# A small fp32 product on TensorE becomes one transpose, with the sums taken by VectorE

## The chip, the cores and the metric

One core of a Trainium2 chip. The metric is the time of one execution on the device in microseconds (us), median of several runs. "The loop" below is the edge loop of the graph attention, which runs once in each of two layers.

## What is computed

`x` has 1250 nodes of 768 features. The reference adds to it a two-layer graph attention over 41250 directed edges and a linear attention, and then a feed-forward block. The change is in the graph attention, whose core is this:

```python
hs_e = hs[src]
e = jax.nn.leaky_relu(hs_e + hd[dst], SLOPE)
logits = jnp.einsum('ehd,hd->eh', e, attn)       # 8 heads of 96
m = jax.ops.segment_max(logits, dst, num_segments=N)
ex = jnp.exp(logits - m[dst])
s = jax.ops.segment_sum(ex, dst, num_segments=N)
out = jax.ops.segment_sum((ex / s[dst])[..., None] * hs_e, dst, num_segments=N)
```

## The kernel before

Edges are sorted by destination and cut into tiles of 128; four tiles make a **macro**, and there are 91 macros in a layer. For every macro the kernel gathers four tiles of source rows by indirect DMA, turns them (six chunks of 128 features, four tiles each) and adds the destinations' rows on TensorE in PSUM (`turn_chunk`), takes the relu on ScalarE (`bend`, one 128x512 activation per chunk), joins three pairs of chunks on VectorE (`join`), sums over the features of each head on TensorE (`sum_heads`), and scans over the edges on VectorE (`scan_left`, `scan_right`, `shift`) to subtract a running maximum. The shifted logits are turned back (`turn_back`), ScalarE takes their exponential (`weights`), VectorE spreads them into a masked matrix (`spread_out`), and TensorE multiplies that with the gathered rows (`messages`). VectorE adds the result to the running sums of the destination blocks (`add_total`, two instructions for each of the four tiles).

A running maximum may rise between macros. By how much is the column `rise` of 128 partitions: a partition is tile j times 32 plus a head's place, h // 4 times 4 plus h % 4. ScalarE makes `drop` from it (`drops`), TensorE sums and places it for the partitions that `sums` has (`sum_drops`), and ScalarE takes the exponentials of it (`factors`, four activations of 128x2), by which `add_total` scales what was summed so far. `quarter_mask` is a 128x8 mask of zeros and ones, `head_rows` a 128x128 one.

The loop is pipelined by hand into slots: in a slot, TensorE does the messages of macro i, `sum_heads` and what follows for macro i + 1 (`head`), and turns the chunks of macro i + 2 (`turn`). In each layer 88 of the slots run as 22 rounds of a loop of four, the rest is written out. TensorE's order in a slot is fixed: messages, heads (products of chunk 3, of chunk 5, of chunk 4), chunks 0, 1, 2, `turn_back`, chunks 3, 4, `sum_drops`, `turn_linear`, chunk 5. ScalarE's is: relu 0, linear, relu 1, `weights`, `drops`, relu 2, 3, 4, `factors`, relu 5. VectorE's is: three joins, one tile's additions, the scans and the shift, three tiles' additions, `spread_out`. Engines meet through semaphores that count; among these, `sum_heads` waits before its second product, that of chunk 5, for relu 5.

Of the kernel before, what the change touches and what calls it, by code (L numbers as in the profile page):

```python
# [15 lines left out]
P = 128  # L16
# [13 lines left out]
HM = 4  # L30
HH = H // HM
# [327 lines left out]
JOINED = ((0, 1), (2, 3), (1, 4))  # L359
JOINED_HEADS, ALONE, LEAST = (3, 4), 5, 3  # L360
LOOPS = (NM - TAIL) // UNROLL
assert LOOPS * UNROLL + TAIL == NM
# [14 lines left out]
def macro(i, k):  # L377
# [5 lines left out]
              "turned_back", "weights_ready", "spread_ready", "totalled", "added", "firsts", "merge_ready", "merged",  # L383
              "merge_seen", "joined", "linear_ready")
AT_LISTS = ("local_loaded", "flags_loaded", "lines_loaded", "gathered")
# [20 lines left out]
def attend(layer, ahead, sums, table, places, lines, run_flags, src_index, first_dst, still_first, block_of, sum_of,  # L406
           ident, head_rows, quarter_mask, dst_rows, sems, nc, **_):

    with ExitStack() as ctx:
# [3 lines left out]
        def psum(name):  # L413
# [8 lines left out]
        right, shifted = sb("at_right", [P, P]), sb("at_shifted", [P, P])  # L422
        drop = sb("at_drop", [P, G * HH])
        weight = sb("at_weight", [P, G * H])
# [15 lines left out]
        (cleared, index_ready, index_seen, turned_done, bent, heads_done, scanned, raised, dropped, turned_back, weights_ready,  # L440
         spread_ready, totalled, added, firsts, merge_ready, merged, merge_seen, joined, linear_ready) = sems[0:len(AT_SIGNALS)]
        local_loaded, flags_loaded, lines_loaded, gathered = (
# [11 lines left out]
        with nc.Block() as block:  # L454
# [71 lines left out]
            def _(act):  # L526
# [6 lines left out]
                def drops(m, b):  # L533
                    act.wait_ge(scanned, m * SCANS + (SCANS + 2))
                    act.activation(rise[:], left[(b + 1) % 2][:, P - 1:P], ACT.Identity, bias=right[:, 0:1], scale=-1.0)
                    act.activation(first_maxima[:, bass.ds(m, 1)], right[:, 0:1], ACT.Copy).then_inc(raised, 1)
                    act.wait_ge(raised, m + 2)
                    act.activation(drop[:], quarter_mask[:, 0], ACT.Relu, scale=rise[:]).then_inc(dropped, 1)

# [5 lines left out]
                def factors(m, b):  # L545
                    act.wait_ge(turned_back, 2 * m + 2)
                    for j in range(G):
                        act.activation(factor[b % 2][:, j, :], back[:, P + j * HH:P + (j + 1) * HH], ACT.Exp,  # L548
                                       scale=first_dst[:, bass.ds(m * G + j, 1)]).then_inc(weights_ready, 1)
# [37 lines left out]
            def _(pe):  # L587
# [46 lines left out]

                def sum_drops(m):
                    weights_there, drop_there = count(m * EXPS + (EXPS + 1)), count(m + 1)
                    pe.wait_ge(weights_ready, weights_there)
                    pe.wait_ge(dropped, drop_there)
                    pe.matmul(back[:, P:P + G * HH], head_rows[:], drop[:], start=True, stop=True).then_inc(turned_back, 1)  # L639

# [21 lines left out]
                def slot(turn, head, message, at, coming=None):  # L662
                    if message:
                        for pair in range(2):
                            messages(message[0], message[1], pair)
                    if head:
                        sum_heads(head[0], head[1])
                    if turn:
                        turn_chunk(*turn, at, 0)
                        turn_chunk(*turn, at, 1)  # L670
                        turn_chunk(*turn, at, 2)
                    if head:
                        turn_back(head[0])
                    following = None
                    if turn:
                        turn_chunk(*turn, at, 3)
                        if coming:
                            following = coming(turn[0] + 1)
                        turn_chunk(*turn, at, 4)
                    if head:  # L680
                        sum_drops(head[0])
                    if turn:
                        turn_linear(turn[0])
                        turn_chunk(*turn, at, 5)
                    return following
# [19 lines left out]
            def _(dve):  # L705
# [22 lines left out]
                def spread_out(m, b, round):  # L728
# [3 lines left out]
                                      weight[:].rearrange("p (j h) -> p j h", j=G).unsqueeze(3).broadcast_to([P, G, H, S]), ALU.mult).then_inc(spread_ready, 1)  # L732

                def add_total(m, b, j, at):
                    dve.wait_ge(totalled, m * 2 + (j // 2 + 1))
# [8 lines left out]
                def slot(head, message):  # L744
                    if message:
                        at = places_of(nc, mybir.EngineType.DVE, sum_of, message[0], 1, NS + G - 1)
                    if head:
                        for k in range(len(JOINED)):
                            join(head[0], k)
                    if message:  # L750
                        for j in range(1):
                            add_total(message[0], message[1], j, at)
# [4 lines left out]
                    if message:  # L757
                        for j in range(1, G):
                            add_total(message[0], message[1], j, at)
# [1633 lines left out]
```

## Time and profile before

| | |
|---|---|
| time, median of 3 runs | 2142.82 us (2141.51 to 2144.17) |
| profiled execution, its own time | 2140.68 us |
| its span, first to last instruction | 2138.9 us |
| TensorE matmul busy | 2052.9 us, 96% |
| VectorE busy | 1641.7 us, 77% |
| ScalarE busy | 1160.9 us, 54% |
| GpSimd busy | 975.4 us, 46% |
| mean granted TensorE clock | 0.986 |

The span lies within the execution's own time; the 1.8 us between are before the first and after the last instruction. PE is TensorE's matmul, PEld its weight load, DVE is VectorE, ACT ScalarE, POOL GpSimd. A busy share is a mean over all stages: how long a slot of the loop takes is read from the start of an instruction in one slot to the start of the same one in the next.

### The profile page before, as it was taken

The page shows a single profiled execution, that of the slowest core. Times are in us where ns is not written, and L with a number is a line of the kernel's source. Part 1 is how long each engine was busy: PE and PEld are TensorE (multiplying, and loading weights), DVE is VectorE, ACT ScalarE, POOL GpSimd, SP SyncE. Part 2 cuts the span into 40 slices and gives each one's busy share as a digit, 9 for nine tenths or more (in the row PEclk, how much of TensorE's full clock was granted, in tenths as well). Part 3 has the DMA queues.
Part 4 walks back from the last instruction along what each step waited for, and adds up shares of the span by engine and source line. Part 5 has one row for each costly group of instructions (what it writes and reads, how often), then busy time and mean ns, then how long its engine had stood idle before and what let it go on. Part 6 is the DMA issues. An engine that isn't in the chain of part 4 may idle for free. (4 is left out here: it accounts for less than half of the span.)

```text
span 2138.9 us, 85423 instructions
## 1 busy us (share of the span) xinstructions
PE 2052.9 (96%) x29551; PEld 1665.6 (78%) x29552; DVE 1641.7 (77%) x3719; ACT 1160.9 (54%) x3113; POOL 975.4 (46%) x1023
## 2 busy tenths in 40 slices
PE   7999999998999999999998899899999999999798
PEld 4665555555899999999997555599999999999676
DVE  5545883554799999999998764499999999999883
ACT  2101210014677777777775413477777777777583
POOL 0000010110677777777772311277777777777020
PEclk9999999999999999999999999999999999999899
DMA  6000233683888888888884224488888888888511
GB/s 202 1 0 16 74 105 121 185 208 78 248 270 269 274 270 270 271 268 272 270 273 136 87 91 128 131 264 272 269 270 272 271 263 275 271 266 275 185 49 51
DMA packets 184668, 415.48 MB, mean 194 GB/s; under 512 B 59967, under 2 KB 122693, under 8 KB 184557
## 3 DMA queue, kind: packets, MB, share of 16 engines
q0 software_dynamic: 59584, 298.64, 45.0%
q1 hardware_dynamic: 105899, 98.97, 14.9%
q10 hardware_dynamic: 19104, 16.79, 2.8%
q8 instruction: 50, 0.82, 0.2%
q14 instruction: 31, 0.25, 0.0%
HBM read 379.72 MB, written 23.13 MB: 188 GB/s over the span
## 5 line engine op out<-in xcount | busy, mean ns | idle before, releaser
L531 ACT ACTIVATE at_relu<-at_turned,ah_attn_size 128x512 f32<-128x512 f32 x1092 | 713.9, 688 | 306.4 <-PE at_turned L605 286.6
L507 POOL DMA_INDIRECT at_rows<-table,ah_index x360 | 425.2, 1181 | 175.9 <-POOL ah_index L495 71.7
L507 POOL DMA_INDIRECT ah_room<-table,ah_index x352 | 422.8, 1201 | 164.7 <-POOL ah_index L495 65.7
L711 DVE SCALAR_TENSOR_TENSOR at_relu<-at_relu,ah_pair_sign 128x512 f32<-128x512 f32 x546 | 376.8, 744 | 8.2 <-ACT at_relu L531 8.2
L741 DVE SCALAR_TENSOR_TENSOR sums<-sums,at_factor,at_total 128x97 f32 x1456 | 358.8, 308 | 5.4 <-PE at_total L647 2.2
L601 PE MATMUL at_turned<-ident,ah_room 128*128 128x128 f32 x2208 | 341.1, 277 | 19.3 <-PEq L1702 19.0
L601 PE MATMUL at_turned<-ident,at_rows 128*128 128x128 f32 x2160 | 331.0, 276 | 0.1
L601 PEld LDWEIGHTS at_turned<-ident,ah_room 128*128 128x128 f32 x2208 | 243.3, 142 | 40.5 <-issue 40.3
L601 PEld LDWEIGHTS at_turned<-ident,at_rows 128*128 128x128 f32 x2160 | 236.3, 141 | 19.9 <-issue 19.9
L731 DVE TENSOR_TENSOR at_spread<-at_lined,at_weight 128x1024 f32<-128x1024 bf16 x182 | 221.5, 1217 | 2.8 <-ACT at_weight L542 2.8
L605 PE MATMUL at_turned<-ah_place,dst_rows 96*128 96x128 bf16 x2208 | 215.7, 219 | 0.0
L605 PE MATMUL at_turned<-at_place,dst_rows 96*128 96x128 bf16 x2160 | 209.9, 219 | 0.1
L605 PEld LDWEIGHTS at_turned<-ah_place,dst_rows 96*128 x2208 | 171.8, 98 | 6.6
L605 PEld LDWEIGHTS at_turned<-at_place,dst_rows 96*128 x2160 | 167.0, 97 | 6.5 <-issue 0.4
L717 DVE TENSOR_TENSOR_SCAN at_left<-at_flags,at_left,at_heads 128x128 f32<-128x128 bf16 x182 | 87.2, 479 | 98.4 <-PE at_heads L617 96.9
L617 PE MATMUL at_heads<-at_relu,ah_sign_mask 128*8 128x128 f32 x4368 | 153.6, 273 | 1.2 <-ACT at_relu L531 0.5
L647 PE MATMUL at_total<-ah_room,at_spread 128*32 128x100 f32 x5888 | 145.4, 250 | 0.9 <-issue 0.2
L647 PE MATMUL at_total<-at_rows,at_spread 128*32 128x100 f32 x5760 | 143.6, 252 | 1.4 <-DVE at_spread L731 1.4
L647 PEld LDWEIGHTS at_total<-ah_room,at_spread 128*32 128x32 f32 x5888 | 125.3, 110 | 13.0 <-issue 7.4
L548 ACT ACTIVATE at_factor<-at_back,first_dst 128x2 f32<-128x2 f32 x728 | 132.4, 281 | 1.3 <-PE at_back L639 1.3
L647 PEld LDWEIGHTS at_total<-at_rows,at_spread 128*32 128x32 f32 x5760 | 123.5, 110 | 10.8 <-DVE at_spread L731 1.6
L617 PEld LDWEIGHTS at_heads<-at_relu,ah_sign_mask 128*8 128x8 f32 x4368 | 107.8, 89 | 9.7 <-ACT at_relu L531 1.1
(315 smaller groups left out, 2884.7 us busy)
## 6 DMA issues: line engine op xcount, KB each, us to landing
at_flags<-run_flags SPq DMA_DIRECT2D x182, 64.0 KB
dst_rows<-pr_parts SPq DMA_DIRECT2D x76, 144.0 KB, 2.7
ah_place<-places SPq DMA_DIRECT2D x92, 96.0 KB
at_place<-places SPq DMA_DIRECT2D x90, 96.0 KB
table<-ah_room SPq DMA_DIRECT2D x20, 400.0 KB, 3.2
ah_room<-table,ah_index POOLq DMA_INDIRECT x368
at_lined<-lines SPq DMA_DIRECT2D x182, 32.0 KB
at_rows<-table,ah_index POOLq DMA_INDIRECT x360
```

The source lines that it names most:

```text
L507: pool.indirect_dma_start(rows[b][:, j, :], None, table, bass.IndirectOffsetOnAxis(index[b][:, j:j + 1], 0)).then_inc(gathered[b], 16)
L531: act.activation(relu[c][:], turned[chunk(b, c)][:], ACT.Relu, scale=attn_size[:, c:c + 1]).then_inc(bent, 1)
L548: act.activation(factor[b % 2][:, j, :], back[:, P + j * HH:P + (j + 1) * HH], ACT.Exp, scale=first_dst[:, bass.ds(m * G + j, 1)]).then_in ...
L601: pe.matmul(into[j], rows[b][:, j, c * P:(c + 1) * P], ident[:], is_transpose=True, start=j == 0, stop=False)
L605: last = pe.matmul(into[j], dst_rows[0:SP_ROWS, bass.ds(at[j], 1), c * P:(c + 1) * P].rearrange("p o d -> p (o d)"), place[b][:, j * P:(j ...
L617: last = pe.matmul(head_row(j), sign_mask[:, c - LEAST, :], relu[c][:, j * P:(j + 1) * P], start=False, stop=final)
L647: last = pe.matmul(part(j)[h % HM * S:(h % HM + 1) * S, h // HM, :], spread[:, j, h, :], rows[b][:, j, :].rearrange("p (g h r) -> p h g r" ...
L711: dve.scalar_tensor_tensor(relu[c][:], relu[from_][:], pair_sign[:, c:c + 1], relu[c][:], ALU.mult, ALU.add).then_inc(joined, 1)
L717: dve.tensor_tensor_scan(left[b % 2][:], flags[b][:, 0, :], heads[:, 0:P], left[(b + 1) % 2][:, P - 1:P], ALU.add, ALU.max).then_inc(scann ...
L731: dve.tensor_tensor(spread[:], lined[b % 2][:].unsqueeze(2).broadcast_to([P, G, H, S]), weight[:].rearrange("p (j h) -> p j h", j=G).unsqu ...
L741: dve.scalar_tensor_tensor(into[:, k], into[:, k], factor[b % 2][:, j, k:k + 1], part(j)[:, k, 0:HW], ALU.mult, ALU.add).then_inc(added, 1)
```

## The change

`drop` grows from 128x8 to 128x128 (it now lies in `iota_row`, a 128x128 tile of fp32 that is there already), `sum_drops` becomes `turn_drops`, a transpose of it, and a new VectorE instruction, `fold_drops`, adds groups of four columns of the transposed tile in PSUM and writes 128x8 numbers, `fold`, to SBUF. `factors` now waits for that (`folded`) and reads `fold` in SBUF, where it read `back` in PSUM. In VectorE's slot the new instruction stands between the first and the second join, and the second tile's additions move ahead of the scans.

```diff
+AHEAD_OF_SCANS = 2
...
-        drop = sb("at_drop", [P, G * HH])
+        drop, fold = iota_row, sb("at_fold", [P, G, HH])
...
-                    act.activation(drop[:], quarter_mask[:, 0], ACT.Relu, scale=rise[:]).then_inc(dropped, 1)
+                    act.activation(drop[:], head_rows[:], ACT.Relu, scale=rise[:]).then_inc(dropped, 1)
...
                 def factors(m, b):
-                    act.wait_ge(turned_back, 2 * m + 2)
+                    act.wait_ge(folded, m + 1)
                     for j in range(G):
-                        act.activation(factor[b % 2][:, j, :], back[:, P + j * HH:P + (j + 1) * HH], ACT.Exp,
+                        act.activation(factor[b % 2][:, j, :], fold[:, j, :], ACT.Exp,
                                        scale=first_dst[:, bass.ds(m * G + j, 1)]).then_inc(weights_ready, 1)
...
-                def sum_drops(m):
+                def turn_drops(m):
                     weights_there, drop_there = count(m * EXPS + (EXPS + 1)), count(m + 1)
                     pe.wait_ge(weights_ready, weights_there)
                     pe.wait_ge(dropped, drop_there)
-                    pe.matmul(back[:, P:P + G * HH], head_rows[:], drop[:], start=True, stop=True).then_inc(turned_back, 1)
+                    pe.transpose(back[:, P:2 * P], drop[:], ident[:]).then_inc(turned_back, 1)
...
+                def fold_drops(m):
+                    dve.wait_ge(turned_back, 2 * m + 2)
+                    dve.tensor_reduce(fold[:], back[:, P:2 * P].rearrange("p (j k g) -> p j k g", j=G, g=HM)[:, :, 0:HH, :], AX.X, ALU.add).then_inc(folded, 1)
...
                     if head:
-                        for k in range(len(JOINED)):
-                            join(head[0], k)
+                        join(head[0], 0)
                     if message:
-                        for j in range(1):
+                        fold_drops(message[0])
+                    if head:
+                        join(head[0], 1)
+                        join(head[0], 2)
+                    if message:
+                        for j in range(AHEAD_OF_SCANS):
                             add_total(message[0], message[1], j, at)
                     if head:
                         scan_left(*head)
                         scan_right(head[0], head[1])
                         shift(head[0])
                     if message:
-                        for j in range(1, G):
+                        for j in range(AHEAD_OF_SCANS, G):
                             add_total(message[0], message[1], j, at)
```

TensorE, in one of the loop's slots, between chunks 4 and 5: the product with `at_drop` as its moving side (fp32, two passes in the trace), before,

```order
L605 MATMUL at_turned_0<-at_place_0,dst_rows 128x128
L637 ISA
L639 MATMUL at_back<-at_drop,head_rows 128x8 [waits at_dropped,at_weights_ready]
L612 MATMUL at_heads<-ident,at_linear 128x128 [waits at_linear_ready]
L599 REGISTER_ALU
```

and now, with the same waits:

```order
L606 MATMUL at_turned_0<-at_place_0,dst_rows 128x128
L638 ISA
L640 MATMUL at_back<-ident,iota_row 128x128 [waits at_dropped,at_weights_ready]
L613 MATMUL at_heads<-ident,at_linear 128x128 [waits at_linear_ready]
L600 REGISTER_ALU
```

One instruction stands in the place of one; nothing else moves on TensorE.

VectorE, in one of the loop's slots, from the first join to the first scan (`at_relu_0` are the relu tiles, `sums` the running sums), before,

```order
L711 SCALAR_TENSOR_TENSOR at_relu_0<-at_relu_0,ah_pair_sign 128x512 [waits at_bent]
L708 REGISTER_ALU
L711 SCALAR_TENSOR_TENSOR at_relu_0<-at_relu_0,ah_pair_sign 128x512 [waits at_bent]
...
L711 SCALAR_TENSOR_TENSOR at_relu_0<-at_relu_0,ah_pair_sign 128x512 [waits at_joined]
...
L741 SCALAR_TENSOR_TENSOR sums<-sums,at_factor_0,at_total_0 128x97
L741 ISA
L741 SCALAR_TENSOR_TENSOR sums<-sums,at_factor_0,at_total_0 128x97
L714 REGISTER_ALU
L717 SCALAR_TENSOR_TENSOR at_left_0<-at_flags_0,at_left_0,at_heads 128x128 [waits at_flags_loaded3,at_raised,at_heads_done]
```

and now:

```order
L712 SCALAR_TENSOR_TENSOR at_relu_0<-at_relu_0,ah_pair_sign 128x512 [waits at_bent]
L736 ISA
L737 TENSOR_REDUCE at_fold<-at_back 128x8 [waits at_turned_back]
L709 REGISTER_ALU
L712 SCALAR_TENSOR_TENSOR at_relu_0<-at_relu_0,ah_pair_sign 128x512 [waits at_bent]
...
L746 SCALAR_TENSOR_TENSOR sums<-sums,at_factor_0,at_total_0 128x97
L746 ISA
L746 SCALAR_TENSOR_TENSOR sums<-sums,at_factor_0,at_total_0 128x97
L746 ISA [waits at_totalled]
L746 SCALAR_TENSOR_TENSOR sums<-sums,at_factor_0,at_total_0 128x97
L746 ISA
```

The reduction stands behind the first join, and four additions instead of two stand ahead of the scan; behind the shift there are four instead of six.

## Rows read from the trace of the kernel before

**Rows 1.** Page: busy time by engine; the costliest groups of lines.

```profile
PE 2052.9 (96%) x29551; PEld 1665.6 (78%) x29552; DVE 1641.7 (77%) x3719; ACT 1160.9 (54%) x3113; POOL 975.4 (46%) x1023
...
L617 PE MATMUL at_heads<-at_relu,ah_sign_mask 128*8 128x128 f32 x4368 | 153.6, 273 | 1.2 <-ACT at_relu L531 0.5
```

**Rows 2.** Timeline of TensorE, one slot: start us, length us, instructions.

```profile
705.33 0.28 PE L633 MATMUL at_back<-ident,at_shifted 128*128 128x128 f32 x1
705.45 0.60 PE L601 MATMUL at_turned<-ident,ah_room 128*128 128x128 f32 x4
...
706.78 0.34 PE L639 MATMUL at_back<-at_drop,head_rows 128*128 128x8 f32 x2
706.97 0.31 PE L612 MATMUL at_heads<-ident,at_linear 128*128 128x128 f32 x1
707.12 0.27 PE L601 MATMUL at_turned<-ident,ah_room 128*128 128x128 f32 x1
...
709.27 0.49 PE L617 MATMUL at_heads<-at_relu,ah_sign_mask 128*8 128x128 f32 x9
...
709.27 0.84 PE L617 MATMUL at_heads<-at_relu,ah_sign_mask 128*8 128x128 f32 x24
```

**Rows 3.** Timeline of ScalarE, the same slot.

```profile
704.78 0.25 ACT L554 ACTIVATE at_linear<-ah_room 128x32 f32<-128x32 f32 x1
704.94 0.67 ACT L531 ACTIVATE at_relu<-at_turned,ah_attn_size 128x512 f32<-128x512 f32 x1
705.65 0.20 ACT L542 ACTIVATE at_weight<-at_back 128x32 f32<-128x32 f32 x1
705.74 0.29 ACT L535 ACTIVATE at_columns<-at_left,at_right 128x1 f32<-128x1 f32 x1
705.94 0.19 ACT L536 ACTIVATE at_first_maxima<-at_right 128x1 f32 x1
706.16 0.30 ACT L538 ACTIVATE at_drop<-quarter_mask,at_columns 128x8 f32<-128x8 f32 x1
706.36 1.83 ACT L531 ACTIVATE at_relu<-at_turned,ah_attn_size 128x512 f32<-128x512 f32 x3
708.07 0.73 ACT L548 ACTIVATE at_factor<-at_back,first_dst 128x2 f32<-128x2 f32 x4
708.65 0.73 ACT L531 ACTIVATE at_relu<-at_turned,ah_attn_size 128x512 f32<-128x512 f32 x1
```

**Rows 4.** Timeline of the loop's first slot, where TensorE waits for relu 5.

```profile
544.47 0.41 PE L617 MATMUL at_heads<-at_relu,ah_sign_mask 128*8 128x128 f32 x8
545.12 0.28 PE L617 MATMUL at_heads<-at_relu,ah_sign_mask 128*8 128x128 f32 x1 [0.25 <-ACT at_relu L531]
...
543.61 1.47 ACT L531 ACTIVATE at_relu<-at_turned,ah_attn_size 128x512 f32<-128x512 f32 x2
```

**Rows 5.** Timeline, next slot, around the loop's branch: TensorE, ScalarE, VectorE.

```profile
712.09 0.28 PE L633 MATMUL at_back<-ident,at_shifted 128*128 128x128 f32 x1
...
716.09 0.41 PE L617 MATMUL at_heads<-at_relu,ah_sign_mask 128*8 128x128 f32 x8
...
715.41 0.73 ACT L531 ACTIVATE at_relu<-at_turned,ah_attn_size 128x512 f32<-128x512 f32 x1
...
712.81 1.22 DVE L731 TENSOR_TENSOR at_spread<-at_lined,at_weight 128x1024 f32<-128x1024 bf16 x1
```

**Rows 6.** Timeline of ScalarE behind the loop, and in the last stage (out of PSUM).

```profile
1159.84 0.28 ACT L535 ACTIVATE at_columns<-at_left,at_right 128x1 f32<-128x1 f32 x1
1160.03 0.19 ACT L536 ACTIVATE at_first_maxima<-at_right 128x1 f32<-128x1 f32 x1
...
2050.95 0.86 ACT L2145 ACTIVATE fi_hidden<-fi_hidden_ps,fi_bias 128x128 f32<-128x128 f32 x3
...
L2145 ACT ACTIVATE fi_hidden<-fi_hidden_ps,fi_bias 128x128 f32<-128x128 f32 x30 | 8.8, 362 | 7.3 <-PE fi_hidden_ps L2204 7.2
```

**Rows 7.** Timeline of VectorE, the slot of rows 2; then the groups by shape.

```profile
705.94 1.22 DVE L731 TENSOR_TENSOR at_spread<-at_lined,at_weight 128x1024 f32<-128x1024 bf16 x1
707.08 2.07 DVE L711 SCALAR_TENSOR_TENSOR at_relu<-at_relu,ah_pair_sign 128x512 f32<-128x512 f32 x3
709.13 0.54 DVE L741 SCALAR_TENSOR_TENSOR sums<-sums,at_factor,at_total 128x97 f32 x2
710.28 0.48 DVE L717 TENSOR_TENSOR_SCAN at_left<-at_flags,at_left,at_heads 128x128 f32<-128x128 bf16 x1 [0.61 <-PE at_heads L617]
...
L711 DVE SCALAR_TENSOR_TENSOR at_relu<-at_relu,ah_pair_sign 128x512 f32<-128x512 f32 x546 | 376.8, 744 | 8.2 <-ACT at_relu L531 8.2
L741 DVE SCALAR_TENSOR_TENSOR sums<-sums,at_factor,at_total 128x97 f32 x1456 | 358.8, 308 | 5.4 <-PE at_total L647 2.2 <-DVE at_relu L794 0.7 <-issue 0.2
...
L1076 DVE TENSOR_REDUCE quarter_mask<-ident 128x8 f32<-128x32 f32 x1 | 0.2, 176 | 0.0
```

More of the change, by code:

```diff
@@ L383 @@
               "turned_back", "weights_ready", "spread_ready", "totalled", "added", "firsts", "merge_ready", "merged",
-              "merge_seen", "joined", "linear_ready")
+              "merge_seen", "joined", "linear_ready", "folded")
 AT_LISTS = ("local_loaded", "flags_loaded", "lines_loaded", "gathered")
@@ L406, in attend @@
 def attend(layer, ahead, sums, table, places, lines, run_flags, src_index, first_dst, still_first, block_of, sum_of,
-           ident, head_rows, quarter_mask, dst_rows, sems, nc, **_):
+           iota_row, ident, head_rows, quarter_mask, dst_rows, sems, nc, **_):
     with ExitStack() as ctx:
@@ L440, in attend @@
         (cleared, index_ready, index_seen, turned_done, bent, heads_done, scanned, raised, dropped, turned_back, weights_ready,
-         spread_ready, totalled, added, firsts, merge_ready, merged, merge_seen, joined, linear_ready) = sems[0:len(AT_SIGNALS)]
+         spread_ready, totalled, added, firsts, merge_ready, merged, merge_seen, joined, linear_ready, folded) = sems[0:len(AT_SIGNALS)]
         local_loaded, flags_loaded, lines_loaded, gathered = (
@@ L680, in slot @@
                     if head:
-                        sum_drops(head[0])
+                        turn_drops(head[0])
                     if turn:
```

## The prediction

> **What bounds the kernel now.** The page of the profile comes first: TensorE's matmuls are busy for 96% of the span, VectorE for 77%, ScalarE for 54% [rows 1]. So a cut on TensorE looks like the only cut that pays. But a busy share doesn't say how close the others follow behind it, so I read one slot of the loop in the timeline, TensorE's and ScalarE's rows side by side. Reader: look for the place at which TensorE needs something from ScalarE, and how long before that it was there.
>
> From one `turn_back` (705.33 us) to the next (712.09) a slot takes 6.76 us [rows 2, 5], with hardly a gap on TensorE. ScalarE's work in a slot starts from that `turn_back`: its exponential stands at 705.65, directly behind the product's end at 705.33 + 0.28 = 705.61 [rows 2, 3]. From there `weights`, `rise`, the copy of the maxima, `drop`, relu 2, 3 and 4, four factors and relu 5 follow each other without a pause, and relu 5 ends at 708.65 + 0.73 = 709.38 [rows 3]. TensorE needs it at the ninth matmul of `sum_heads`. Nine of these matmuls end 0.49 after 709.27, and one lasts 0.27, so the ninth starts at 709.49 [rows 2]. Relu 5 is there 0.10 us (0.103 by the records' own times) before its use. How much of that is free? In the loop's first slot TensorE does wait for it: relu 5 ends at 543.61 + 1.47 = 545.08 and the matmul starts at 545.12 (0.05 apart, unrounded 0.053) [rows 4]. So **the slack is 0.05 us per slot**: over the whole trace TensorE waits 0.5 us in these groups for ScalarE [rows 1], yet ScalarE is almost a second critical path, from `turn_back` to the ninth matmul of `sum_heads`. The removed product lies on TensorE inside that same stretch.
>
> **The change, part by part.**
>
> TensorE. The product of two passes takes from 706.78 to 706.97, and the linear transpose behind it until 707.12: 0.34 together. A single fp32 transpose, `turn_back`, takes 705.33 to 705.45, 0.12 [rows 2]; two such in a row make 0.24. Saving: 0.10 us per slot (bounds: 0.07 if only the product's own 0.19 shrinks to 0.12, and 0.10), or 18 us over 182 slots if nothing else ended later.
>
> ScalarE, `drop`. It has 128 columns instead of 8. The price of a column: relus of 512 columns start (708.07 - 706.36) / 3 = 0.570 apart, factors of 2 columns (708.65 - 708.07) / 4 = 0.145 apart [rows 3], so 0.425 / 510 = 0.83 ns. The 128-column activations of the last stage confirm it: three take 0.86, one 0.36 in the mean, so they start 0.25 apart [rows 6], and 0.145 + 126 x 0.83 ns = 0.25. So 120 columns more are **+0.10 us**. The 0.20 between `drop` and relu 2 could hide part of it, if register work and not the activation set it: then 0.04 is the low bound. I take 0.10, since the last row of this kind without such work fits as well: `rise` (1 column, SBUF, a per-partition operand) is followed after 0.19 by the copy behind the loop, 0.20 within it [rows 3, 6], the same as behind `drop`.
>
> ScalarE, `factors`. They are as many and as wide as before, but read SBUF instead of PSUM, with a per-partition scale from SBUF. The rows divide by this: `rise`, out of SBUF and with such an operand, keeps the engine 0.185 to 0.20 us for one column [rows 3, 6]; a factor, out of PSUM and with such an operand, 0.145; `weights`, out of PSUM and without one, 0.09 for 32 columns, and the linear copy, out of SBUF and without one, 0.16 for 32 [rows 3]. So SBUF as the source costs some 0.04 to 0.055 more per activation, four times: **+0.16 to +0.22**, low bound 0 (if `rise` owes its spacing to something else). I take 0.18. Against it stands that relu 5 lasts 0.73 behind the factors and 0.67 where nothing is queued closely ahead of it [rows 3]: its start is recorded early while results pile up, and with wider spacing it won't be; -0.04.
>
> The Trainium skill (ScalarE: Activation LUTs, "What ACT_TABLE_LOAD costs") gives 186 ns plus 0.833 ns per column, 93 more for each per-partition operand, and an overlap of 93 between neighbours. By that a factor takes 0.19 wherever it reads. The `rise` row agrees; the factors' own 0.145 doesn't, and the row decides. Taken as it stands the rule would leave the factors' price unchanged, and this is the first rival.
>
> The wait for `folded`. VectorE's first join starts at 707.08, three joins of 0.74 end after 2.07, so they start 0.66 apart: the reduction can start at 707.74. The same shape was reduced once from SBUF in 0.18 [rows 7]; it ends at 707.92. From one engine's end to another's start with register work between I take 0.17 (the heads' products end at 709.27 + 0.84 = 710.11 [rows 2], the scan starts at 710.28 [rows 7]): 708.09. ScalarE reaches the factors at 708.07 + 0.10 for the wider `drop` = 708.17. So the wait is covered by `drop`'s own growth, by 0.08. In the slot after, `spread_out` starts 0.72 behind `turn_back` instead of 0.61 [rows 2, 5, 7], which would use the cover up; but there VectorE was late with its additions, and with four of them behind the shift instead of six (0.23 each: two end after 0.54, one lasts 0.31) it will wait for `weights` alone. Price 0, bounds 0 and 0.1.
>
> VectorE itself. The reduction pushes the next joins by under 0.2, and two additions more stand ahead of the scan. It idles 0.61 there now [rows 7], and the two additions are 0.46. The factors come 0.1 + 0.14 later, so the additions start at about 709.37 instead of 709.13 and leave the engine free at 710.29; but `sum_heads` ends later too, by what TensorE waits. The scan starts where it did, behind `sum_heads`. The joins have 0.3 us and more left before their products. Price 0.
>
> **The sum.** Relu 5 comes 0.10 + 0.18 - 0.04 = 0.24 us later, measured from `turn_back`. An ordinary slot has 0.05 of slack, so it grows by 0.19: TensorE waits 0.29 at the ninth matmul and had saved 0.10. One slot in four, at the loop's branch, has more: relu 5 ends at 716.14, the ninth matmul starts at 716.09 + 0.22 = 716.31, 0.17 apart, 0.12 of it free [rows 5]; it grows by 0.12. A round: 3 x 0.19 + 0.12 = 0.69. 44 rounds: 30 us; the six slots outside add 1, and the few rounds in which TensorE was late in this stretch for other reasons take off 2. **+29 us.** Against the profiled execution's own 2140.7 that is 2169.7. That execution lies 2.1 below the median of the runs shown, 2142.8; against the median I forecast 2172.
>
> **Rivals.**
> First, the factors cost no more out of SBUF than out of PSUM. Relu 5 is late by 0.10 alone; an ordinary slot grows by 0.05, one at the branch shrinks by 0.02: 44 x 0.13 = 6 us, 2148. For it: nothing but `rise` and `drop` price SBUF with an operand at few columns. Against: both rows say the same, with and without register work.
>
> Second, **faster**: ScalarE's growth doesn't reach relu 5 because `drop`'s is hidden in register work and the factors' spacing stays. It is the place of the sum with the hardest cap: TensorE can gain only the slack of 0.05 in an ordinary slot and the full 0.10 at a branch, 44 x 0.25 = 11 us, 2132. It decides when relu 5 is late by under 0.05 in place of 0.24. Against: the slope of 0.83 ns is in three kinds of rows.
>
> Third, the fold is late. If VectorE's reduction of PSUM or its place behind the join costs 0.2 more than I take, all factors start 0.1 later and every slot with them: 18 us more, 2190.
>
> **How the numbers follow.** The forecast (both ScalarE terms, late by 0.16 to 0.32; 2157 to 2186) has 0.65; the first rival 0.15, of which a third lies within 0.2%; the second 0.08, a little of it within 0.2%; the third 0.12. A change of under 0.2% is about what a measurement of this kernel can't tell from none. Faster 0.07, same 0.07, slower 0.86. The range leaves out the second rival and the upper part of the third: 2147 to 2187.
>
> **What would show it.** In the profile after: `drop` at 0.40 us instead of 0.30; factors' starts 0.185 to 0.20 apart, the four taking some 0.85 from first to last end; a wait of TensorE in `sum_heads` on the relu, 0.2 to 0.3 us per slot, 45 us or so in all, where there are 0.5 now; the transpose 0.12 before the linear one; slots of 6.95 instead of 6.76; VectorE no longer late for `spread_out`. Wrong would be: factors 0.145 apart (then the first rival), no wait in `sum_heads` (the second), ScalarE idle ahead of the factors waiting for `fold` (the third), or a scan that starts behind the additions and not behind `sum_heads`.

## The result, and the profile after

| | before | after |
|---|---|---|
| time, median | 2142.2 us (2141.5 to 2144.2, 4 runs) | 2169.6 us (2167.1 to 2169.7, 4 runs) |
| profiled execution, own time / span | 2140.7 / 2138.9 us | 2169.5 / 2167.8 us |
| TensorE / VectorE / ScalarE busy | 96 / 77 / 54% | 95 / 78 / 55% |

The ratio is 1.0123 (95% interval 1.0112 to 1.0135): the changed kernel is 1.2% slower. 2172 was forecast, 29 us up; it is 27. One run of experiment 1 fell into a slow state (2347 us, at a lower granted clock, 0.864); its ratio leaves that run out.

The page after, the busy times and the groups that answer to [rows 1], with the two groups of the changed instructions on ScalarE and the new one on VectorE:

```profile
PE 2068.6 (95%) x29369; PEld 1643.4 (76%) x29370; DVE 1681.7 (78%) x3901; ACT 1201.2 (55%) x3113; POOL 1009.2 (47%) x1023
...
L618 PEld LDWEIGHTS at_heads<-at_relu,ah_sign_mask 128*8 128x8 f32 x4368 | 102.0, 89 | 55.0 <-ACT at_relu L532 46.4
...
L539 ACT ACTIVATE iota_row<-head_rows,at_columns 128x128 f32<-128x128 f32 x182 | 73.2, 402 | 5.9
...
L549 ACT ACTIVATE at_factor<-at_fold,first_dst 128x2 f32<-128x2 f32 x728 | 154.5, 294 | 8.1 <-DVE at_fold L737 8.1
...
L737 DVE TENSOR_REDUCE at_fold<-at_back 128x8 f32<-128x32 f32 x182 | 33.5, 184 | 1.0 <-DVE at_relu L803 1.0
```

The line to look at is the weight load of `sum_heads` (L618): TensorE now waits 46.4 us there for the relu. The same row of the kernel before, and the row of the group's matmuls after, which [rows 1] has for before:

```profile
L617 PEld LDWEIGHTS at_heads<-at_relu,ah_sign_mask 128*8 128x8 f32 x4368 | 107.8, 89 | 9.7 <-ACT at_relu L531 1.1
...
L618 PE MATMUL at_heads<-at_relu,ah_sign_mask 128*8 128x128 f32 x4368 | 186.1, 273 | 9.5 <-ACT at_relu L532 0.5
```

Like is compared with like in the weight loads: 1.1 us before, 46.4 after. The 0.5 that the prediction read stands in the matmuls' row, and it is 0.5 after as well, so that row could not have shown the wait. TensorE's busy time went up in the page though a pass was taken from it. These matmuls are recorded as 273 ns long, before and after, but in an undisturbed group they start closely behind each other and their records overlap. When the ninth comes 0.25 us later, the record of the eighth covers most of the gap, and the group counts as 186.1 us busy instead of 153.6. Busy time alone tells the wrong story.

One ordinary slot, TensorE, from the timeline (answers to [rows 2]):

```profile
709.18 0.28 PE L634 MATMUL at_back<-ident,at_shifted 128*128 128x128 f32 x1
709.30 0.60 PE L602 MATMUL at_turned<-ident,ah_room 128*128 128x128 f32 x4
...
710.63 0.28 PE L640 MATMUL at_back<-ident,iota_row 128*128 128x128 f32 x1
710.74 0.27 PE L613 MATMUL at_heads<-ident,at_linear 128*128 128x128 f32 x1
710.85 0.60 PE L602 MATMUL at_turned<-ident,ah_room 128*128 128x128 f32 x4
...
713.00 0.78 PE L618 MATMUL at_heads<-at_relu,ah_sign_mask 128*8 128x128 f32 x9
...
716.11 0.28 PE L634 MATMUL at_back<-ident,at_shifted 128*128 128x128 f32 x1
```

ScalarE in the same slot (answers to [rows 3]):

```profile
709.50 0.20 ACT L543 ACTIVATE at_weight<-at_back 128x32 f32<-128x32 f32 x1
...
710.01 0.40 ACT L539 ACTIVATE iota_row<-head_rows,at_columns 128x128 f32<-128x128 f32 x1
710.32 1.82 ACT L532 ACTIVATE at_relu<-at_turned,ah_attn_size 128x512 f32<-128x512 f32 x3
712.03 0.84 ACT L549 ACTIVATE at_factor<-at_fold,first_dst 128x2 f32<-128x2 f32 x4
712.77 0.68 ACT L532 ACTIVATE at_relu<-at_turned,ah_attn_size 128x512 f32<-128x512 f32 x1
```

VectorE in the same slot (answers to [rows 7]):

```profile
709.73 1.23 DVE L732 TENSOR_TENSOR at_spread<-at_lined,at_weight 128x1024 f32<-128x1024 bf16 x1 [0.30 <-ACT at_weight L543]
710.87 0.74 DVE L712 SCALAR_TENSOR_TENSOR at_relu<-at_relu,ah_pair_sign 128x512 f32<-128x512 f32 x1
711.53 0.18 DVE L737 TENSOR_REDUCE at_fold<-at_back 128x8 f32<-128x32 f32 x1
711.63 1.41 DVE L712 SCALAR_TENSOR_TENSOR at_relu<-at_relu,ah_pair_sign 128x512 f32<-128x512 f32 x2
713.12 0.99 DVE L746 SCALAR_TENSOR_TENSOR sums<-sums,at_factor,at_total 128x97 f32 x4
714.30 0.48 DVE L718 TENSOR_TENSOR_SCAN at_left<-at_flags,at_left,at_heads 128x128 f32<-128x128 bf16 x1 [0.19 <-PE at_heads L618]
```

Read in this order: from `turn_back` to `turn_back` 709.18 to 716.11, 6.93 us instead of 6.76. The drops' transpose and the linear one take 0.22 (710.63 to 710.85) instead of 0.34, so TensorE did save 0.12. ScalarE reaches relu 2 0.31 behind the start of `drop` instead of 0.21 (0.207 unrounded), and its factors start 0.185 apart ((712.77 - 712.03) / 4) instead of 0.145. Relu 5 ends at 713.45, 4.27 behind `turn_back` instead of 4.05. The ninth matmul of `sum_heads` starts at 713.00 + 0.78 - 0.27 = 713.51, 0.06 (0.053 unrounded) behind relu 5: exactly the distance that [rows 4] showed for the slot in which TensorE waited. The fold ends at 711.71, 0.3 ahead of the factors.

### The profile page after: what moved, and what is told of

Read it like the earlier page. It is cut to its first block and busy times, and to the rows that moved or that the text cites. A ratio compares the mean times of both kernels' runs of the same rounds, so it can differ in the third digit from the quotient of the medians.

```text
span 2167.8 us, 85066 instructions
## 1 busy us (share of the span) xinstructions
PE 2068.6 (95%) x29369; PEld 1643.4 (76%) x29370; DVE 1681.7 (78%) x3901; ACT 1201.2 (55%) x3113; POOL 1009.2 (47%) x1023
## 5 line engine op out<-in xcount | busy, mean ns | idle before, releaser
L532 ACT ACTIVATE at_relu<-at_turned,ah_attn_size 128x512 f32<-128x512 f32 x1092 | 705.2, 680 | 291.9 <-PE at_turned L606 284.2
L508 POOL DMA_INDIRECT at_rows<-table,ah_index x360 | 444.8, 1236 | 172.1 <-issue 82.1
L508 POOL DMA_INDIRECT ah_room<-table,ah_index x352 | 435.4, 1237 | 162.3 <-issue 68.6
L712 DVE SCALAR_TENSOR_TENSOR at_relu<-at_relu,ah_pair_sign 128x512 f32<-128x512 f32 x546 | 391.7, 745 | 9.1 <-ACT at_relu L532 9.1
L618 PE MATMUL at_heads<-at_relu,ah_sign_mask 128*8 128x128 f32 x4368 | 186.1, 273 | 9.5 <-ACT at_relu L532 0.5
L549 ACT ACTIVATE at_factor<-at_fold,first_dst 128x2 f32<-128x2 f32 x728 | 154.5, 294 | 8.1 <-DVE at_fold L737 8.1
L618 PEld LDWEIGHTS at_heads<-at_relu,ah_sign_mask 128*8 128x8 f32 x4368 | 102.0, 89 | 55.0 <-ACT at_relu L532 46.4
```

What stands on the lines that cost most here:

```text
L508: pool.indirect_dma_start(rows[b][:, j, :], None, table, bass.IndirectOffsetOnAxis(index[b][:, j:j + 1], 0)).then_inc(gathered[b], 16)
L532: act.activation(relu[c][:], turned[chunk(b, c)][:], ACT.Relu, scale=attn_size[:, c:c + 1]).then_inc(bent, 1)
L549: act.activation(factor[b % 2][:, j, :], fold[:, j, :], ACT.Exp, scale=first_dst[:, bass.ds(m * G + j, 1)]).then_inc(weights_ready, 1)
L618: last = pe.matmul(head_row(j), sign_mask[:, c - LEAST, :], relu[c][:, j * P:(j + 1) * P], start=False, stop=final)
L712: dve.scalar_tensor_tensor(relu[c][:], relu[from_][:], pair_sign[:, c:c + 1], relu[c][:], ALU.mult, ALU.add).then_inc(joined, 1)
```

## The experiments

All times are medians; ratios are against the kernel before, run beside each. Unless said otherwise a kernel starts from the changed one.

**1. The wide drop alone.** On the kernel before; `drop` is a view of the same 128x128 tile.

```diff
-                    act.activation(drop[:], quarter_mask[:, 0], ACT.Relu, scale=rise[:])
+                    act.activation(drop, over(quarter_mask[:, 0], P // (G * HH)), ACT.Relu, scale=rise[:])
...
-                    pe.matmul(back[:, P:P + G * HH], head_rows[:], drop[:], start=True, stop=True)
+                    pe.matmul(back[:, P:P + G * HH], head_rows[:], drop[:, 0], start=True, stop=True)
```

> The kernel before, with one edit: ScalarE writes drop as 128x128 (the 128x8 mask repeated 16 times), of which TensorE's product reads the first 8 columns. Nothing else changes. My theory (the path turn_back, ScalarE, relu 5, sum_heads bounds the slot, with 0.05 us of slack): drop lasts 0.40, relu 2 starts 0.31 behind it instead of 0.21, relu 5 comes 0.10 later, an ordinary slot grows by 0.05 and one at the loop's branch not at all: about +7 us, 2149 against 2142. Rival (register work hides the wider drop): +0 to 1 us. Rival (only the wait for the fold or VectorE's order costs): no change.

Measured: 2150.0 against 2143.1, ratio 1.0031 (1.0019 to 1.0043). ScalarE's rows:

```profile
706.40 0.40 ACT L538 ACTIVATE iota_row<-quarter_mask,at_columns 128x128 f32<-128x128 f32 x1
706.71 1.82 ACT L531 ACTIVATE at_relu<-at_turned,ah_attn_size 128x512 f32<-128x512 f32 x3
708.42 0.72 ACT L548 ACTIVATE at_factor<-at_back,first_dst 128x2 f32<-128x2 f32 x4
708.99 0.73 ACT L531 ACTIVATE at_relu<-at_turned,ah_attn_size 128x512 f32<-128x512 f32 x1
```

Relu 2 starts 0.31 behind `drop`: the columns' full 0.10 is paid, no register work hides it. The +7 us are those of my theory.

**2. The factors from SBUF alone.** `drop` is 128x8 again and the product stands as before; VectorE copies its 128x8 result. Of the edit, the lines of TensorE and VectorE:

```diff
-                    pe.transpose(back[:, P:2 * P], drop[:], ident[:])
+                    pe.matmul(back[:, P:P + G * HH], head_rows[:], drop[:], start=True, stop=True)
...
-                    dve.tensor_reduce(fold[:], back[:, P:2 * P].rearrange("p (j k g) -> p j k g", j=G, g=HM)[:, :, 0:HH, :], AX.X, ALU.add)
+                    dve.tensor_copy(fold[:], back[:, P:P + G * HH].rearrange("p (j k) -> p j k", j=G))
```

> The changed kernel with the drops as before (128x8, product on TensorE); VectorE copies the product's 128x8 from PSUM to SBUF where the changed kernel adds, and the factors read the copy in SBUF. VectorE's order is the changed one. My theory: factors start 0.185 apart instead of 0.145 (4 x 0.04 = 0.16), relu 5 lasts 0.68 instead of 0.73, so relu 5 comes 0.11 later, an ordinary slot grows by 0.06 and one at the branch hardly: about +8 us, 2150; up to +6 more if the factors now wait for the copy, which has lost the cover of the wider drop. Rival (the source of the factors costs nothing): +0 us but for such a wait.

Measured: 2153.5 against 2143.1, ratio 1.0050 (1.0036 to 1.0064).

```profile
706.00 1.83 ACT L532 ACTIVATE at_relu<-at_turned,ah_attn_size 128x512 f32<-128x512 f32 x3
707.71 0.85 ACT L549 ACTIVATE at_factor<-at_fold,first_dst 128x2 f32<-128x2 f32 x4
708.45 0.68 ACT L532 ACTIVATE at_relu<-at_turned,ah_attn_size 128x512 f32<-128x512 f32 x1
```

The factors follow relu 4 as closely as before (1.71 behind the start of relu 2, as in [rows 3]), so no wait for the copy stands in; they start 0.185 apart. In the loop's slots the source alone costs this: from the first to the last `turn_back` the two layers take 9.3 us more. Some 1.4 us more lie at the ends of the layers (see the wait for the fold below).

**3. The fold in PSUM.** VectorE writes the fold into another part of `back`'s bank.

```diff
-        drop, fold = iota_row, sb("at_fold", [P, G, HH])
+        drop = iota_row
...
+        fold = back[:, 2 * P:2 * P + G * HH].rearrange("p (j k) -> p j k", j=G)
```

> The changed kernel, but VectorE writes the fold to PSUM (another part of the same bank), and the factors read it there. My theory: factors 0.145 apart again, relu 5 0.11 earlier than in the changed kernel; TensorE's saving of 0.12 stays; slots of 6.82: about 2150, 20 us faster than the changed kernel and 7 slower than the kernel before. Rival (the cost is the wait for the fold, or its place in VectorE's queue): no faster than the changed kernel, 2169.

Measured: 2151.0 against 2143.1, ratio 1.0032 (1.0021 to 1.0043); 8 us over the kernel before, where the changed kernel is 27 over it.

```profile
709.36 1.82 ACT L533 ACTIVATE at_relu<-at_turned,ah_attn_size 128x512 f32<-128x512 f32 x3
711.07 0.73 ACT L550 ACTIVATE at_factor<-at_back,first_dst 128x2 f32<-128x2 f32 x4
711.65 0.73 ACT L533 ACTIVATE at_relu<-at_turned,ah_attn_size 128x512 f32<-128x512 f32 x1
```

Same instructions, same waits, same order; only the memory in which the fold's 128x8 numbers lie differs, and it decides: 0.145 apart again, and relu 5 lasts 0.73 again. The rival (a wait for the fold, its place in VectorE's queue) falls as the cause of the 19 us between these two kernels.

**4. TensorE's part alone.** On the kernel before; the rises are left out of the sums.

```diff
-                    pe.matmul(back[:, P:P + G * HH], head_rows[:], drop[:], start=True, stop=True)
+                    pe.transpose(back[:, P:2 * P], head_rows[:], ident[:])
```

> TensorE's part alone: the kernel before, in which TensorE transposes the 128x128 mask in place of the product with drop; ScalarE and VectorE are as before, and the factors read the first columns of that transpose. The rises of the maxima are left out of the sums, so the output isn't the reference's. My theory (TensorE can gain no more than the slack of 0.05 in an ordinary slot, 0.12 at the branch): 12 us faster, 2130. Rival (TensorE alone bounds the slot, 0.12 in each): 21 us faster, 2121.

Measured: 2136.4 against 2143.1, ratio 0.9969 (0.9958 to 0.9980), 7 us faster where 12 were expected and 21 by the rival. The waits of the whole trace:

```profile
PEld at_heads L617 <- ACT at_relu L531: 15.7, 91, 0.5
```

This view counts 91 waits of TensorE for relu 5, where the kernel before had two (1.1 us): the slack of 0.05 is used up, as expected, and an ordinary slot takes 6.71. What I had wrong is the slot at the loop's branch: it stays at about 6.85, and doesn't gain the 0.12 that was expected. Experiments 6 to 12 come back to this.

**5. VectorE's order.** One tile's additions ahead of the scans again.

```diff
-AHEAD_OF_SCANS = 2
+AHEAD_OF_SCANS = 1
```

> The changed kernel with one tile's additions ahead of the scans, as before, instead of two. My theory (VectorE's order isn't on the path that sets the end): no change against the changed kernel, 2169, within 2. Rival (the second tile's additions ahead of the scan delay what follows): faster by up to their 0.46 us per slot.

Measured: 2172.2 against 2142.6, ratio 1.0139 (1.0124 to 1.0155); the changed kernel's own ratio was 1.0123 (1.0112 to 1.0135). The intervals overlap. The order isn't a cause of the loss, and two ahead gain nothing that these runs can tell.

**6. Relu 5 first.** ScalarE takes relu 5 ahead of the factors; one tile's additions ahead of the scans.

```diff
+                        bend(turn[0], turn[1], 5, first)
                     if head:
                         factors(head[0], head[1])
-                    if turn:
-                        bend(turn[0], turn[1], 5, first)
...
-AHEAD_OF_SCANS = 2
+AHEAD_OF_SCANS = 1
```

> The changed kernel with relu 5 ahead of the four factors on ScalarE, and one tile's additions ahead of the scans. My theory: relu 5 ends some 0.75 earlier, far ahead of its use, so TensorE bounds the slot and its 0.12 comes through wherever the loop's branch doesn't take it: 16 us faster than the kernel before, 2127. The factors end 0.7 later, which delays the first additions to 0.3 behind the end of sum_heads; the scan's 0.55 of slack before turn_back covers that. Rival (VectorE is then the bound): slots of 6.8 and more, 2143 or slower.

Measured: 2140.1 against 2142.6, ratio 0.9989 (0.9980 to 0.9998). This is 29 us less than the changed kernel, and the only kernel with the whole computation that is also under the kernel before, by 2.5 us (the interval ends just below 1). Since the order of the additions makes no difference (5), relu 5's lateness was the whole loss. But of the 16 us expected below the kernel before, 2.5 came. `turn_back` of five consecutive slots, and the wait of the whole trace that shows where time is lost:

```profile
706.40 0.28 PE L633 MATMUL at_back<-ident,at_shifted 128*128 128x128 f32 x1
...
713.05 0.28 PE L633 MATMUL at_back<-ident,at_shifted 128*128 128x128 f32 x1
...
720.00 0.28 PE L633 MATMUL at_back<-ident,at_shifted 128*128 128x128 f32 x1
...
726.65 0.28 PE L633 MATMUL at_back<-ident,at_shifted 128*128 128x128 f32 x1
...
733.41 0.28 PE L633 MATMUL at_back<-ident,at_shifted 128*128 128x128 f32 x1
...
PEld at_total L647 <- issue: 13.7, 42, 0.5
```

6.65, 6.95, 6.65, 6.76: two slots in four have the full gain of 0.11, the one at the branch takes 6.95 instead of 6.83, and the fourth 6.76. The 42 waits "for issue" (the profile shows nothing that TensorE waited for) all lie in the slots at the branch, ahead of the messages. A round of four takes 27.0 (medians of the positions: 6.96 + 6.65 + 6.75 + 6.65), against 27.1 before (6.83 + 3 x 6.76). Number 4 comes to the same 27.0 with other slots (6.85 + 3 x 6.71). What is gained in some slots is lost in the others.

**7. One factor activation.** VectorE multiplies by `first_dst`, ScalarE takes one exponential of 128x8.

```diff
-                    for j in range(G):
-                        act.activation(factor[b % 2][:, j, :], fold[:, j, :], ACT.Exp,
-                                       scale=first_dst[:, bass.ds(m * G + j, 1)]).then_inc(weights_ready, 1)
+                    act.activation(factor[b % 2][:], fold[:], ACT.Exp).then_inc(weights_ready, 1)
...
-                    dve.tensor_reduce(fold[:], back[:, P:2 * P]... AX.X, ALU.add).then_inc(folded, 1)
+                    dve.tensor_reduce(fold[:], back[:, P:2 * P]... AX.X, ALU.add).then_inc(summed, 1)
+                    dve.wait_ge(summed, m + 1)
+                    dve.tensor_tensor(fold[:], fold[:], first_dst[:, bass.ds(m * G, G)].unsqueeze(2).broadcast_to([P, G, HH]), ALU.mult).then_inc(folded, 1)
```

> The changed kernel, in which VectorE multiplies the fold by first_dst as well (one 128x8 instruction more, behind the reduction), so that one activation of 128x8 replaces the four factors. My theory: ScalarE's path is shorter by some 0.6, relu 5 ends about 3.65 behind turn_back, TensorE doesn't wait for it: 2127. Rival (the fold's wait costs what the factors give back): 2140 and over.

Measured: 2142.8 against 2142.6, ratio 1.0003 (0.9994 to 1.0012). Relu 5 ends 3.65 behind `turn_back`, as expected, and TensorE doesn't wait for it; but 2127 was expected, and the time is that of before all the same, with the same pattern of slots as in 6 (a round of 27.1). The rival here, a wait for the fold, isn't the reason: relu 5 comes as early as expected.

**8. Both of these.** One tile's additions ahead of the scans.

> Both of these edits together, with one tile's additions ahead of the scans. My theory: TensorE is the bound in each of them already, so the two together give no more than the faster of them, within 3 us. Rival (some of the path is still ScalarE's or VectorE's): faster than both by over 3 us.

Measured: 2145.0 against 2142.6, ratio 1.0010 (1.0001 to 1.0019). That is no better than 6 or 7, and 5 us slower than 6, where at most 3 us apart were expected. One row of its waits:

```profile
PEld at_heads L615 <- DVE at_relu L709: 19.4, 95, 0.3
```

TensorE now waits for VectorE's joins, 19.4 us in 95 slots, where the kernels of 6 and 7 have 0.6 and 0.7 us; its best slots take 6.70 instead of 6.65. So ScalarE's path doesn't hold the rest, but this run can't acquit VectorE. The traces of 6 and 7 can: TensorE waits there neither for the relu nor for the joins in more than a few slots, and a round takes 27.0 and 27.1.

**9 to 11. A longer loop for TensorE.** Eight slots per round, TensorE alone: on 6, on the kernel before, and on the changed one.

```diff
-                with pe.Fori(0, LOOPS) as i:
+                with pe.Fori(0, LOOPS // 2) as i:
                     at = carried_blocks()
-                    for k in range(UNROLL):
-                        at = slot(macro(i, k + 2), macro(i, k + 1), macro(i, k), at, blocks if k < UNROLL - 1 else carry_blocks)
+                    for n in range(2 * UNROLL):
+                        two = [(i * (2 * UNROLL) + k, k % UNROLL, i * 2 + k // UNROLL) for k in (n + 2, n + 1, n)]
+                        at = slot(*two, at, blocks if n < 2 * UNROLL - 1 else carry_blocks)
```

> Of the kernel with relu 5 ahead of the factors, TensorE's loop alone has eight slots per round instead of four, so half the branches; the instructions are the same. In that kernel the slots away from the branch are at 6.65, those at the branch at 6.96 (0.20 of it ahead of the messages), and a round of four takes 27.0 as before the change. Theory A (a branch costs TensorE a fixed time, which now shows): 22 branches fewer per layer, 0.2 to 0.35 each: 9 to 15 us faster than with four, 2125 to 2131. Theory B (TensorE can't start instructions faster than this in the mean, wherever the branch is): no change, 2140.

> The kernel before, with TensorE's loop of eight slots per round. Slots at the branch take 0.07 more than the others there: theory A gives 2 to 3 us faster, 2140; theory B no change.

> The changed kernel, with TensorE's loop of eight slots per round. All its slots take 6.93, the ones at the branch too, since ScalarE's path from turn_back to relu 5 sets them: no change, 2170, under both theories of the branch. If the branch did set the slots there: 2 us faster and more.

Measured: 2309.1, 2306.0 and 2327.7 against 2143.0; ratios 1.0789 (1.0769 to 1.0808), 1.0783 (1.0762 to 1.0803), 1.0865 (1.0849 to 1.0881). All three expectations were wrong by 158 us and more, in the same way, so these runs don't answer what they were made for. From number 10: the queue that carries instructions (packets, MB, share); the messages behind one long wait and, a slot later, without one; the window right behind that wait, whose last three numbers are the mean granted clock, DMA share and GB/s; and all such waits:

```profile
q8 instruction: 293, 4.80, 0.9%
...
801.12 2.90 PE L647 MATMUL at_total<-ah_room,at_spread 128*32 128x100 f32 x64 [5.61 <-issue]
...
809.60 1.58 PE L647 MATMUL at_total<-ah_room,at_spread 128*32 128x100 f32 x64
...
801.10:805.00 3.90, 3.88 (x89) 3.51 (x90) 0.54 (x2) 0.00 (x0) 0.09 (x1) 0.59 0.04 14
...
PEld at_total L647 <- issue: 99.2, 23, 5.9
```

The queue has 293 packets instead of 50, 4.80 MB instead of 0.82. The 243 more are 11 for each of the 22 rounds (11 in each layer), and the kernel has 23 waits of 99 us in all ahead of the messages' weight loads in which nothing of the profile holds TensorE. A second loss follows: after the 5.6 us of idleness TensorE's granted clock is 0.59 of full speed in the mean of the next 3.9 us, and the 64 matmuls of the messages last 2.90 us instead of 1.58. It is so behind 19 of the 20 waits of over 1 us, some 25 us in all for the messages alone. The Trainium skill (Runtime: NRT & Kernel Launch, "Instruction fetch mechanics") says that TensorE's instruction memory holds 128 KiB and is filled in blocks of 16 KiB, and that a taken branch whose target isn't in the current window must fetch it first. The traces agree with the blocks and the fetch: the packets are 16 KB each (3.98 MB / 243), and a loop twice as long costs them in each round. A run with six slots, which would find the limit, wasn't made.

**12. Without TensorE's address registers.** On 6: destination blocks 0 to 3 for every macro, so the register work ahead of each of 24 matmuls per slot and the loads of the numbers are left out of TensorE's program. The destinations' rows are then the wrong ones, so the output isn't the reference's; the matmuls are the same. Of the edit, the main line:

```diff
-                        last = pe.matmul(into[j], dst_rows[0:SP_ROWS, bass.ds(at[j], 1), c * P:(c + 1) * P]...
+                        last = pe.matmul(into[j], dst_rows[0:SP_ROWS, j:j + 1, c * P:(c + 1) * P]...
```

> The kernel with relu 5 ahead of the factors, and TensorE without its address registers: it takes destination blocks 0 to 3 for every macro instead of reading the blocks' numbers, so about half of its rows in the loop's order (register work ahead of each matmul with the destinations' rows, and the loads of the numbers) are left out; matmuls and their data sizes are the same, the output isn't the reference's. With relu 5 first a round of four slots takes 27.0 us, though two of the four run at 6.65. If TensorE's register work sets that mean (the rest of its instructions wait behind it): all slots at 6.65, a round at 26.6, 17 us faster than the same kernel with the registers, 2123. If the loop's branch or the supply of matmuls sets it: 2135 to 2140, with slots at the branch still at 6.9.

Measured: 2122.3 against 2142.2, ratio 0.9904 (0.9888 to 0.9921).

```profile
707.46 0.28 PE L633 MATMUL at_back<-ident,at_shifted 128*128 128x128 f32 x1
...
714.11 0.28 PE L633 MATMUL at_back<-ident,at_shifted 128*128 128x128 f32 x1
...
720.76 0.28 PE L633 MATMUL at_back<-ident,at_shifted 128*128 128x128 f32 x1
...
727.40 0.28 PE L633 MATMUL at_back<-ident,at_shifted 128*128 128x128 f32 x1
...
734.05 0.28 PE L633 MATMUL at_back<-ident,at_shifted 128*128 128x128 f32 x1
```

As expected: all four positions are at 6.65, the one at the branch too, and the waits for issue ahead of the messages are gone. The work on the addresses, register instructions and the loads of the numbers together, set the mean of 6.75 per slot. The branch by itself costs nothing that the slots show, for it is still there. That the loss shows mainly at the branch because TensorE's matmuls run ahead of their register work until they catch up with it fits these rows, but no run shows it. The matmuls themselves run at 6.65 once the transpose has replaced the product.

## Why the prediction was right

**The path.** That ScalarE follows TensorE with 0.05 us of slack, from `turn_back` to the ninth matmul of `sum_heads`, is confirmed by the 0.053 between relu 5 and that matmul in the slots after, by the 46.4 us of waits there (I forecast some 45; before it was 1.1 in the same row, not 0.5), by experiment 4, where TensorE alone ran into relu 5, and by 6, where moving relu 5 took the whole loss away.

**The terms.** `drop`: +0.10 forecast, 0.10 measured, alone (1) and together. Factors: +0.18 forecast, 0.16 measured (4 x 0.04), 0.12 net of relu 5's shorter duration against 0.14. Relu 5 later by 0.22 instead of 0.24. TensorE's saving: 0.12 instead of 0.10, of no use, since TensorE waits it out. An ordinary slot: 6.93 measured, 6.95 forecast. The loop's slots account for 24.3 us of the 28.9 between the two profiled spans: from the first `turn_back` to the last of a layer 611.7 and 611.1 us before, 623.6 and 623.5 after. So the loop's term, forecast at 29, was 24: an ordinary slot grew by 0.17 and not 0.19, and one at the branch, forecast to grow by 0.12, took 6.90 in the mean before (its median is 6.83) and takes 6.94 now. The other 4.6 lie outside. 1.4 of them are the change's (see the wait for the fold), and the sum had no term for them. The remaining 3.2 lie ahead of the loop, between the layers and behind them, where nothing was changed (first `turn_back` at 547.7 and 549.6); the experiments' traces scatter there by 2 us as well. So the path and its terms were right, but that the total came within 2 us is in part luck: 5 us too much in the loop met 5 us outside it.

**The rival on the factors' source.** I gave 0.15 to factors that cost the same from either memory. Experiments 2 and 3 settle it against that: 0.185 from SBUF, 0.145 from PSUM, with the rest equal. The Trainium skill (Perfetto Trace Analysis, "Optimizing Scalar/DVE Operations") gives ScalarE about 93 ns of access overhead on SBUF and 51 on PSUM. The difference, 42 ns, is the 40 that the traces show. The prediction didn't weigh this.

**The wait for the fold** cost nothing in the loop's slots, and VectorE was no longer late for `spread_out`, both as written. The cover was larger than thought, 0.3 between the fold's end and the first factor, since `spread_out` starts 0.55 behind `turn_back`, not 0.61, once nothing queues ahead of it. In the last slot of each layer, outside the loop, the wait does cost something, against the price of 0 in the prediction. There VectorE does the layer's closing work on the maxima first, and the fold stands behind that. The first layer's end, before (two lines) and after:

```profile
1161.09 0.72 ACT L548 ACTIVATE at_factor<-at_back,first_dst 128x2 f32<-128x2 f32 x4 [0.54 <-PE at_back L639]
1165.02 1.98 DVE L741 SCALAR_TENSOR_TENSOR sums<-sums,at_factor,at_total 128x97 f32 x8 [0.72 <-DVE at_relu L794]
...
1178.17 0.19 DVE L737 TENSOR_REDUCE at_fold<-at_back 128x8 f32<-128x32 f32 x1 [0.51 <-DVE at_relu L803]
1178.40 0.85 ACT L549 ACTIVATE at_factor<-at_fold,first_dst 128x2 f32<-128x2 f32 x4 [3.94 <-DVE at_fold L737]
1179.45 1.89 DVE L746 SCALAR_TENSOR_TENSOR sums<-sums,at_factor,at_total 128x97 f32 x8 [1.09 <-ACT at_factor L549]
```

The factors wait 3.94 us for the fold, and VectorE's last additions wait for the factors: they start 6.27 us behind the layer's last `turn_back` instead of 5.64, and in the second layer 6.47 instead of 5.65, 1.4 us in all.

**The faster rival's cap** was too high: 11 us for TensorE's part alone, measured 7. The step that failed is "the full 0.10 at a branch". The slot there is long because of the register work and loads that number 12 takes away, not because of a delay that a shorter matmul would shorten. It had no part in the forecast, but it decides what a repair is worth: experiments 6 to 8 each freed ScalarE's path and came back to 2140 to 2145, not to 2127.

What stays open: how much of TensorE's limit of 27.0 us per round is the time of the register instructions and how much that of the loads of the blocks' numbers, one set of which stands right at the branch, since 12 took away both. Fetching the instructions is hardly it: the instruction queue has 50 packets in the whole of number 6 and 48 in number 12.

## What to carry to other kernels

Before work moves from the busiest engine to an idler one, measure how far behind the idler one is on the path between two points where they meet, not how busy it is: here 54% busy hid 0.05 us of slack in a slot of 6.8. Of small activations count how many, and from where they read: four of 128x2 are priced by their number and by the memory of their source, and one wide one by its columns as well. And what another engine waits for next can be moved ahead of what it doesn't wait for (relu 5 ahead of the factors): here that gave back 29 us, all that the change had cost.

## What the runs showed of the hardware

- An activation of 128x2 with a per-partition operand keeps ScalarE 0.185 us when it reads SBUF and 0.145 when it reads PSUM (numbers 2 and 3); the recorded length of the activation behind such ones changes with it (0.68 and 0.73), so spacings price such work, not lengths.
- TensorE's work on address registers can bound the loop: 6.75 us per slot in the mean of the four positions with it (number 6), 6.65 without (number 12), though two slots in four run at 6.65 with it. The loss shows at two places of a round, 0.31 at the branch, there as "issue" (42 waits, 13.7 us), and 0.1 two slots later.
- Doubling the body of TensorE's loop cost 163 us (number 10): 243 more instruction packets of 16 KB, and about 7 us in each of 22 rounds. TensorE's granted clock fell as well: 0.59 in the 3.9 us behind one such wait, and over the whole span 0.961 instead of 0.986.
